# Feed-forward stage: pairwise head lengths on GpSimd, one normalising instruction replaced, and a new instruction order

## The reference, cut to what matters

```python
def attn_layer(x, Wqkv, qs, ksc, Wo):
    q, k, v = jnp.split(x @ Wqkv, 3, -1)          # 16 heads of 64
    q = l2norm(q) * qs                            # t / max(|t|, 1e-12), head by head
    k = l2norm(k) * ksc
    q = q * cos * scale + rotate_half(q) * sin * scale
    k = k * cos / scale + rotate_half(k) * sin / scale
    return local_attention(q, k, v) @ Wo          # softmax over a window of 32, 8 * q k

def ffn_layer(x, g, bln, W1, b1, W2, b2):
    xn = (x - mu) / jnp.sqrt(var + 1e-05) * g + bln
    a, gate = jnp.split(xn @ W1 + b1, 2, -1)      # 341 each
    return a * jax.nn.gelu(gate) @ W2 + b2

for i in range(6):
    x = attn_layer(shift_tokens(x), ...) + x
    x = ffn_layer(shift_tokens(x), ...) + x
```

## Time and profile before

| | before |
|---|---|
| median of 3 runs | 3090.07 us (3087.32 to 3096.23) |
| the profiled execution's own time | 3090.18 us |
| its span in the trace | 3088.4 us |
| PE busy over the span | 2621.0 us (85%) |
| PEld busy | 1544.8 us (50%) |
| DVE busy | 2661.1 us (86%) |
| ACT busy | 2258.9 us (73%) |
| POOL busy | 2366.2 us (77%) |
| first `rotated` of the feed-forward part | 2116.7 us |

### The profile page before, as it was taken

The page is one execution under the profiler, slowest core; times in us unless marked ns, Lnnn a source line. Parts: engine busy times, 40 slices in busy tenths (PEclk is TensorE's granted clock), DMA queues, the critical chain, the costliest instruction groups (busy, mean ns, idle before and its releaser), DMA issues.

```text
span 3088.4 us, 51905 instructions
## 1 busy us (share of the span) xinstructions
PE 2621.0 (85%) x12394; PEld 1544.8 (50%) x12457; DVE 2661.1 (86%) x7326; ACT 2258.9 (73%) x4818; POOL 2366.2 (77%) x2544
## 2 busy tenths in 40 slices
PE   4888888878878888888888887996999999999997
PEld 2333333434434434333433334873666666666665
DVE  3999999999999999999999997335899999999996
ACT  3777777777777777777777775335888888888886
POOL 5777777777777777777777776005999999999994
PEclk9999999999999999999999999887999999999998
DMA  5333343333333333333343334000001010101000
GB/s 132 76 73 71 75 71 73 72 73 74 69 75 75 68 75 75 68 75 75 69 75 71 72 74 110 26 1 1 1 0 39 0 39 0 39 0 39 0 0 8
DMA packets 368022, 163.08 MB, mean 53 GB/s; under 512 B 285166, under 2 KB 298228, under 8 KB 367220
## 3 DMA queue, kind: packets, MB, share of 16 engines
q1 hardware_dynamic: 367988, 162.65, 25.6%
HBM read 156.81 MB, written 5.80 MB: 53 GB/s over the span
## 4 chain that ended last, share of the span: by engine, by line
DVE 32%; PE 24%; issue 20%; POOL 15%; ACT 6%; DMA 1%; POOLq 1%; SPq 1%; DVEq 0%; ACTq 0%
PE bank L1475 9%; POOL qk L712 8%; PE bank L1539 5%; DVE bank L1115 4%; PE bank L1490 4%; DVE bank L1110 3%; ACT qkv_w L796 3%; DVE sq L1090 3%; DVE bank L1090 3%; POOL rs L721 3%; DVE fix_trace L1181 2%; ACT qkv_w L819 2%; POOL qk L727 2%; DVE sq L1173 2%; DVE qkv_w L1115 1%
## 5 line engine op out<-in xcount | busy, mean ns | idle before, releaser
L626 POOL TENSOR_TENSOR kT<-upto,xT 128x512 f32<-128x512 f32 x260 | 270.2, 1040 | 379.6 <-PE bank L1480 379.5
L1115 DVE TENSOR_REDUCE bank<-qkv_w 128x2 f32<-128x768 f32 x512 | 465.9, 955 | 88.1 <-ACT qkv_w L819 70.1
L1475 PE MATMUL bank<-diag_h,w_part 128*128 128x512 f32 x1024 | 374.1, 487 | 161.4 <-DVE bank L1110 161.4
L1115 DVE TENSOR_REDUCE qkv_w<-qkv_w 128x4 f32<-128x1536 f32 x256 | 448.0, 1750 | 49.5 <-ACT qkv_w L812 32.3
L812 ACT COPY qkv_w<-bank 128x512 f32<-128x512 f32 x258 | 221.4, 858 | 253.4 <-PE bank L1475 253.4
L1475 PE MATMUL bank<-diag_x,w_part 128*128 128x512 f32 x1032 | 385.7, 496 | 12.7 <-DMA diag_x<-diag_ring 12.6
L1475 PEld LDWEIGHTS bank<-diag_h,w_part 128*128 128x128 f32 x1024 | 184.6, 190 | 409.8 <-issue 386.0
L640 POOL TENSOR_TENSOR diag_h<-eye,part 128x512 fp32r<-128x512 f32 x384 | 388.6, 1040 | 0.0
L1490 PE MATMUL bank<-qT,wh 128*128 128x256 f32 (+1 forms) x768 | 255.4, 468 | 151.9 <-DVE qT L1097 151.0
L721 POOL TENSOR_TENSOR rs<-rs,halfs 128x8 f32<-128x8 f32 x192 | 366.2, 1907 | 16.0
L1719 PE MATMUL bank<-qkv_w,xsT 128*128 (+1 forms) x576 | 310.6, 622 | 10.0 <-DVE rot_s L1330 7.5
(11 more groups left out here) (241 smaller groups left out, 6594.0 us busy)
## 6 DMA issues: line engine op xcount, KB each, us to landing
diag_x<-diag_ring SPq DMA_DIRECT2D x259, 512.0 KB, 6.6
qkv_w<-in_L_ffn_Wqkv SPq DMA_DIRECT2D x6, 1536.0 KB
diag_ring<-X SPq DMA_DIRECT2D x264, 4.0 KB, 5.6
diag_ring<-o_fin SPq DMA_DIRECT2D x8, 512.0 KB, 7.7
o_w<-in_L_ffn_Wo SPq DMA_DIRECT2D x6, 512.0 KB
w<-in_L_ffn_W SPq DMA_DIRECT2D x6, 341.0 KB
b<-in_L_ffn_b SPq DMA_DIRECT2D x6, 341.0 KB
w<-in_L_ffn_W SPq DMA_DIRECT2D x6, 128.0 KB
```

Source lines behind the costliest of these rows:

```text
L626: pool.tensor_tensor(tri[n][:, rows, :], upto[:].unsqueeze(1).to_broadcast([P, 4, D]), src[:, rows].unsqueeze(2).to_broadcast([P, 4, D]), ...
L1115: return dve.tensor_reduce((pre, bias_at[0])[n][:, a:b], chain[n][:, a:b, :], AX_X, ALU.add)
L1475: return pe.matmul(dst, w_part[:, n, w], diag[n][:, d, a:b, :].rearrange("p n k -> p (n k)"), start=False, stop=True, skip_group_check=True)
```

## The change

It has three parts. On GpSimd, `unit_length` takes two chunks at once: one maximum and one power of 128x16 where there were two of 128x8 each; it waits for both chunks' head sums. On VectorE, the first half of the normalised x (L1409) is written by `scalar_tensor_tensor`, with 1/deviation as a second tensor input broadcast along the row, in place of `tensor_scalar` with two scalars. And the written-out order of the blocks in a slot is another one on all four engines. No block is added or dropped otherwise, and every wait is the same, except that the two chunks' counts become one. Empty lines are left out of the diff.

```diff
@@ -204,7 +204,7 @@
         rot_s = sb("rot_s", [P, 2, BANK])
         ss = sb("ss", [P, 4, 8])
         rs = sb("rs", [P, 4, 8])
-        halfs = sb("halfs", [P, 8])
+        halfs = sb("halfs", [P, 2, 8])
         eps = sb("eps", [P, 1])
         warm = sb("warm", [P, 2])
         qk = sb("qk", [P, 4, BANK])
@@ -711,15 +711,16 @@
                                  for r in (qk[:, c, :], rot_c[:, c % 2, :], rot_s[:, c % 2, :]))
                     pool.tensor_tensor(o, c_, s_[:, :, ::-1, :], ALU.add).then_inc(rot_sum, 1)
-                def unit_length(c):
-
-                    eight = value(pool, 8 * i)
-                    heads_summed = value(pool, four + (c + 1))
+                def unit_length(pair):
+
+                    at = slice(2 * pair, 2 * pair + 2)
+                    heads_summed = value(pool, four + (2 * pair + 2))
                     pool.wait_ge(pool_up, 1)
                     pool.wait_ge(ss_ready, heads_summed)
-                    link(pool.tensor_scalar(rs[:, c, :], ss[:, c, :], 1e-24, None, ALU.max), rs_ready, eight + (2 * c + 1))
-                    link(pool.tensor_tensor(rs[:, c, :], rs[:, c, :], halfs[:, 0:8], ALU.pow),
-                         rs_ready, eight + (2 * c + 2))
+                    link(pool.tensor_scalar(rs[:, at, :], ss[:, at, :], 1e-24, None, ALU.max), rs_ready,
+                         four + (2 * pair + 1))
+                    link(pool.tensor_tensor(rs[:, at, :], rs[:, at, :], halfs[:], ALU.pow),
+                         rs_ready, four + (2 * pair + 2))
                 def scaled(c):
@@ -732,7 +733,7 @@
                     pool.wait_ge(var_ready, i - 1)
                     link(pool.tensor_tensor(rstd[:, 0:1], mv[:, 1:2], eps[:], ALU.add), ln_link, i - 1)
-                    pool.tensor_tensor(rstd[:, 1:2], rstd[:, 0:1], halfs[:, 0:1], ALU.pow).then_inc(rstd_ready, 1)
+                    pool.tensor_tensor(rstd[:, 1:2], rstd[:, 0:1], halfs[:, 0, 0:1], ALU.pow).then_inc(rstd_ready, 1)
                 def add_bias():
                     half = place(pool, i - 2)[2]
@@ -742,19 +743,17 @@
                     four = value(pool, 4 * i)
                 if new:
                     rotated(0)
+                    rotated(1)
                     unit_length(0)
                     scaled(0)
-                    rotated(1)
+                    rotated(2)
+                    scaled(1)
+                    rotated(3)
                     unit_length(1)
-                    scaled(1)
-                    rotated(2)
-                    unit_length(2)
+                if mid:
+                    deviation()
+                if new:
                     scaled(2)
-                if mid:
-                    deviation()
-                if new:
-                    rotated(3)
-                    unit_length(3)
                     scaled(3)
                 if mid:
                     add_bias()
@@ -995,44 +994,44 @@
                     act.copy(hgT[0:FI - 256, 2, :], bank[0:FI - 256, 7, 2 * T:3 * T]).then_inc(hgT_copied, 1)
                 if score:
+                    turned(0)
                     turned(1)
-                    turned(0)
                 if new:
                     square(0)
+                if mid:
+                    probs(0)
+                if ahead:
+                    bring(i + 1, 1 - par)
+                if mid:
+                    probs(1)
+                if new:
                     square(1)
-                if mid:
-                    probs(0)
-                    probs(1)
+                if old:
+                    normed()
                 if score:
                     turned(2)
-                if old:
-                    normed()
+                    turned(3)
                 table(ACT.Gelu, 1)
-                if score:
-                    turned(3)
                 if new:
                     square(2)
                 if mid:
                     probs(2)
-                if new:
-                    square(3)
-                if mid:
-                    probs(3)
                 if old:
                     gelu()
                 table(ACT.Exp, 2)
+                if new:
+                    square(3)
+                if mid:
+                    probs(3)
                 if score:
                     exp_of_rows()
-                if mid:
-                    attended(1)
-                if ahead:
-                    bring(i + 1, 1 - par)
-                if mid:
-                    attended(0)
-                if new:
-                    values(0)
                 if old:
                     hidden()
+                if mid:
+                    attended(0)
+                    attended(1)
+                if new:
+                    values(0)
                 if ahead:
                     shifted(i + 1, 1 - par)
                 if score:
@@ -1406,7 +1405,8 @@
                 def norm():
                     dve.wait_ge(rstd_ready, i - 1)
-                    dve.tensor_scalar(xn[:, 0:64], mine[:, 0:64], mv[:, 0:1], rstd[:, 1:2], ALU.subtract, ALU.mult)
+                    dve.scalar_tensor_tensor(out=xn[:, 0:64], in0=mine[:, 0:64], scalar=mv[:, 0:1],
+                                             in1=rstd[:, 1:2].to_broadcast([P, 64]), op0=ALU.subtract, op1=ALU.mult)
                     dve.tensor_scalar(xn[:, 64:128], bank[:, 6, 0:64], mv[:, 0:1], rstd[:, 1:2], ALU.subtract,
                                       ALU.mult).then_inc(xn_ready, 1)
@@ -1417,25 +1417,28 @@
                     squares(1)
                 if score:
                     maximum(0, s_max)
+                if old:
+                    gate_bias()
+                if score:
                     subtract()
                 if old:
-                    gate_bias()
                     value_bias()
                 if new:
                     rotate(2)
+                if old:
+                    gated()
+                if new:
+                    squares(2)
+                    rotate(3)
                 if score:
                     maximum(1, s_less)
-                if old:
-                    gated()
-                if new:
-                    squares(2)
+                if new:
+                    squares(3)
                 if score:
                     denominators()
-                if new:
-                    rotate(3)
-                    squares(3)
-                if score:
                     reciprocals(0)
+                if old:
+                    add_hidden()
                 if mid:
                     add_attended()
                 if score:
@@ -1444,12 +1447,9 @@
                     statistics()
                 if score:
                     reciprocals(1)
-                if old:
-                    add_hidden()
+                    normalise(1)
                 if mid:
                     norm()
-                if score:
-                    normalise(1)
             slots(dve, UNITS, 4, slot)
             dve.wait_ge(a_kept, NB)
@@ -1818,48 +1818,48 @@
                     half_k = place(pe, i - 3)[2]
                     w1_k, w2_k = one(w1, half_k), w2[:, bass.ds(half_k, 1)]
-                if new:
-                    project(0)
                 if score:
                     turn_qk(1)
                     turn_qk(0)
+                    masked(0)
+                if new:
+                    project(0)
+                if mid:
+                    probs(0)
+                    probs(1)
                 if new:
                     project(1)
-                if mid:
-                    probs(1)
-                if score:
-                    masked(0)
-                if mid:
-                    probs(0)
                 if score:
                     all_scores(0)
-                    turn_qk(2)
                 if old:
                     turn_normed()
-                if new:
-                    project(2)
                 if score:
+                    turn_qk(2)
                     turn_qk(3)
                 if old:
                     widen(0)
-                if new:
+                if mid:
+                    probs(2)
+                if new:
+                    project(2)
                     project(3)
                 if mid:
-                    probs(2)
+                    probs(3)
                 if old:
                     widen(1)
                 if mid:
-                    probs(3)
+                    values(0)
                 if score:
                     masked(1)
                     all_scores(1)
-                if mid:
-                    values(1)
-                    values(0)
                 if new:
                     project(4)
                 if old:
                     turn_hidden()
+                if mid:
+                    values(1)
+                if old:
+                    narrow()
                 if ahead:
                     turn_next()
                 if mid:
@@ -1868,8 +1868,6 @@
```

(57 more changed lines are left out.)

## The result

The change costs 6.5 us, where a gain of 23 was forecast: 3096.24 us median (3089.62 to 3099.09, 20 runs) against 3089.72 (3083.34 to 3096.23, 20 runs), a ratio of 1.0019 with a 95% interval of 1.0012 to 1.0025. The interval excludes 1, so the small loss is real; it is within the 9 us that the prediction called no change, and just above its range's upper end of 3096. The profiled execution took 3097.05 us, its span is 3095.2.

A forecast was written before the change was run, and what follows sets the result against it. GpSimd bounds the old kernel at 19.44 us a slot; a loop through three engines then sets 18.95. 45 slots save 22 us, the first three gain some 4, the last three lose some 2.5: about 3067 us, range 3045 to 3096.

The forecast's parts named there:

- GpSimd paces before, and ceases to: GpSimd sets the old pace, 19.44 us a slot, and falls to 17.0, below TensorE's 18.8.
- Part 2 costed at nothing: VectorE's new L1409 is still held by GpSimd's scaled(2): no gain; bounds 0.8 us a slot gained, 0.2 lost.
- end to end come to 18.6: TensorE's old blocks, laid in the new order, sum to 18.6 us a slot.
- The loop of 18.95: Tightest loop, through VectorE, GpSimd and TensorE: (a), (b) and (c) together set the new slot at 18.95 us.
- (a): From add_attended to VectorE's next rotate(0), through the statistics and GpSimd's deviation: 5.29 us.
- (c): From TensorE's project(4) to add_attended, with values(1) and narrow now between: 5.66 us.
- (b): On VectorE, from rotate(0) to the end of rotate(2): 8.0 us.
- Rival A: TensorE alone bounds, with L1409 not held: 18.6 us a slot, 3051 us; chance 0.18.
- Rival B: No change: waits missed by the hand layout, 0.4 us a slot, eat the gain; 3085 us; chance 0.14.
- Rival C: Slower: masked(0), now heading TensorE's list, waits for ScalarE's exp_of_heads; 20.1 us a slot, 3118 us; chance 0.15.
- Rival D: Slower: GpSimd's long power holds VectorE's normalise(0) to its end; 20.5 us a slot, 3136 us; chance 0.05.

The follow-up runs named there:

- e3: The kernel before, with half of the first scores (heads 4 to 7) left out on TensorE: 3087.48 us, slot 19.48 us.
- e2: The kernel after, with half of the first scores (heads 4 to 7) left out on TensorE: 3073.81 us, slot 19.18 us.
- e4: The kernel after, with tensor_scalar put back at L1409: 3092.99 us, slot 19.62 us.
- e16: The kernel of e14 with the old operations (128x8 maxima and powers, tensor_scalar), only the order kept: 3061.44 us, slot 18.97 us.
- e9: The kernel after, with project(2) moved ahead of widen(0) on TensorE: 3074.75 us, slot 19.25 us.
- e13: The kernel after, with shift_up called at the beginning of TensorE's next slot, so slots change behind project(5): 3080.25 us, slot 19.30 us.
- e14: The kernel after, with the TensorE moves of e9 and e13 together: 3061.11 us, slot 18.98 us.
- e15: The kernel of e14 with half of the first scores (heads 4 to 7) left out: 3062.45 us, slot 18.87 us.
- e6: The kernel after, with narrow moved behind shift_up on TensorE and add_hidden moved on VectorE: 3112.42 us, slot 20.10 us.
- e7: The kernel after, with widen(0) moved one block later on TensorE, behind probs(2): 3106.25 us, slot 19.89 us.

## Why the prediction was wrong

The forecast sized the loop of three engines well, and took too short a list for TensorE, which is what paces. Step by step:

- **GpSimd paces before, and ceases to.** Right: e3 against e2. Two readings on the way there were off. The 1.0 us a slot of the earlier trace rows is a wait of TensorE's weight loads (PEld); its matmuls waited 0.2 in every other slot, 5.1 us in 21 times. And 0.6 of 19.44 us caps the gain at 3% of a slot, which is 27 us or 0.9% of the kernel's time.
- **Part 1.** Right in size: power 128x16 took 2.94 (2.95 forecast), the maximum 0.26 (0.30), and GpSimd has time to spare: it waits 1.1 us a slot for the variance and 0.7 for the rotations. `deviation` was held by `normalise(1)` as laid, if for a little less than 1.11: in turn L735 took 1.23 (1.04 more than alone) or L736 took 1.40 (0.85 more).
- **Part 2 costed at nothing.** Right: L1408 takes 1.05 and ends with `scaled(2)`, within 0.1; in the last slots, where GpSimd has no `scaled`, it takes 0.47. `tensor_scalar` in its place (e4) takes 1.02. e4 and e16 found no difference in the slot.
- **TensorE's blocks "end to end come to 18.6".** This step failed; they take 19.62. It was the sum of the earlier trace rows with its waits taken out, carried over to an order in which the neighbours are others. The experiments split the missing 1.02 us. 0.37 is the time at `widen(0)`, taken back by e9: the old list asked ScalarE earlier and had a `project` between. 0.32 is the change of slot with too little work ahead of it, taken back by e13: the old list changed slots behind `narrow`, 0.72 us of work (2632.20 to 2632.92 in the earlier trace rows). The last 0.34 is the blocks' own: without any gap they come to 18.94. The timelines of the kernel before and of e14, start to start, place it at the new neighbours: `values(0)` and `values(1)`, now apart, take 2.05 together instead of 1.90; `project(1)` 0.95 instead of 0.86 ahead of the scores; `widen(1)` 0.67 instead of 0.58 ahead of `values(0)`; `turn_normed` and `narrow` 0.06 more each; `turn_next` 0.1 less. The two savings that the prediction took off, 0.1 each, were there.
- **The loop of 18.95.** It did not decide in the kernel after, where 0.74 us lay between the end of `rotate(2)` (2609.32) and `project(4)` (2610.06), instead of 0.14 in e15, but it was sized right. (a) was laid at 5.29 and took 5.27 (2615.72 to 2620.99) and 5.02 in turn, (c) at 5.66 and took 5.66 (2610.06 to 2615.72), (b) at 8.0 and took 8.09 in e15. With TensorE's gaps closed and half of its first scores left out it measures 18.87. e14, which leaves nothing out, is at 18.98 and 3061, inside the forecast's own 18.75 to 19.2 and 3058 to 3078; it took two moves on TensorE's list that the forecast did not have.
- **Rival A** (18.6, TensorE alone) had the right engine and the wrong price, by the same sum; its condition, an L1409 that isn't held, didn't come true. **Rival B** (waits that a layout by hand misses) is nearest to what came true. But it put 0.4 us a slot on crossings between engines and came to 19.35, while two thirds of what was missed (the 0.32 and the 0.34) lay inside TensorE's own list. **Rival C** fell: from `turn_qk(1)` past the masks to `project(0)` pass 1.36 us, and 1.31 in e14, and no wait for `exp_of_heads` recurs there. (The mask at 2618.03 is the second of two, the first has no record; the same holds for the one of 2617.11 in the earlier trace rows, and the prediction's 2616.9 allows for it.)
- **Rival D** fell: `normalise(0)` took 1.22 inside a power of 2.93. The two rows, of GpSimd and of VectorE in the kernel after:

```profile
2613.84 2.93 POOL L722 TENSOR_TENSOR rs<-rs,halfs 128x16 f32<-128x16 f32 x1
```

```profile
2615.93 1.22 DVE L1363 TENSOR_TENSOR prob<-prob,rden 128x1024 f32<-128x1024 f32 x1
```

By the rule of the Trainium skill, SBUF — State Buffer, "SBUF: two separate sides" (whichever starts first has the shared port pair for the whole instruction), L1363 could not have begun before 2616.77; it began 0.84 us earlier and was not lengthened. The other way round the trace agrees with the rule: L735 of `deviation`, started beside a running `normalise(1)`, ended with it (2619.10 and 2619.05).

## What to carry to other kernels

When an engine's list is reordered by hand, what it waited for is not the only thing to move: every short block that asks another engine for something needs enough independent work between it and the block that uses the answer. Here the answer took 1.4 us: 1.04 us of work in between were too little, and 1.90 (e9) enough. The place where a slot or a loop turn ends needs such work too; 0.17 us were too little and 0.86 enough. A sum of the old list's blocks hides this cover, so sum them with their new neighbours. A block that waits for nothing is the right one to put into a gap (e9, e13); one that itself covers an answer only moves the gap (e6, e7).

## What was unexpected

- **The price of a loop's return depends on the body.** With a body of two slots the return costs TensorE about 0.4 us more than a change of slot inside it (0.68 against 0.30); with six slots 3.9 us pass before the first matmul, and the slot is 6.8 us longer, of which 3.0 are matmuls at the lower clock that follows the stop. The program code that is loaded again in each turn goes with it; that it is the cause is likely and not shown.
- **A change of slot costs time of its own**: from `shift_up` to `turn_qk(1)` pass 0.30 us where `shift_up` alone takes 0.17, and nothing is measurable where the change lies behind 0.86 of work.
- **GpSimd's power and VectorE's multiplication pass each other** when the power came first, even with 2.93 us of it, but not the other way round.
